# Routing two to four iterations sooner, and the first expert tiles between the last cross-attention iterations, in a one-core decoder layer

## The chip, the cores and the metric

One core of one Trainium2 chip. The metric is the device time of one execution in microseconds. Its engines run their own instruction streams and meet at semaphores: TensorE (PE), VectorE (DVE), ScalarE (ACT), GpSimd (POOL), and SyncE (SP), which here only issues transfers.

## The reference

64 sequences of 64 tokens and width 128 (4096 tokens) pass through causal self-attention (16 heads of 64, one key/value head), cross-attention to a context of width 96, and a mixture of 8 experts of which each token uses 2; each step is followed by a residual sum and a layer norm. The part the change touches:

```python
scores_BSN = jnp.einsum('bsd,nd->bsn', x, Wr) + br
w_BSN = jax.nn.softmax(scores_BSN, axis=-1)
_, idx_BSK = jax.lax.top_k(scores_BSN + biases_N[None, None, :], K)
val_BSK = jnp.take_along_axis(w_BSN, idx_BSK, axis=-1)
val_BSK = val_BSK / jnp.sum(val_BSK, axis=-1, keepdims=True)
...
h_NM2H = jnp.einsum('md,ndh->nmh', x_MD, Wl1) + bl1[:, None, :]
a_NMH, b_NMH = (h_NM2H[..., :H], h_NM2H[..., H:])
y_NMD = jnp.einsum('nmh,nhd->nmd', jax.nn.silu(a_NMH) * b_NMH, Wl2) + bl2[:, None, :]
...
y_MD = jnp.einsum('mn,nmd->md', ew_MN, y_NMD)
```

## The kernel before

The tokens are 32 tiles of 128 (T = 32). A first pass does self-attention tile by tile, a second cross-attention, software-pipelined: in iteration i of `cross` (35 iterations, CROSS_END = T + 3) the engines work on the scores of tile i-1, the probabilities and value product of tile i-2, and the residual and norm of tile i-3. Queries and keys are made for two tiles at once in even iterations, the value side in odd ones. Each engine has its own `cross(i, p)`, and the order of calls in it is the order on that engine. TensorE's (lines 1658 to 1704) goes: first half of the scores (`b_s`), transposes of the probabilities (`b_pT`), products for the next tiles, second half of the scores, value product (`b_y`), routing, more products.

Routing is done in eight groups of four tiles (G = 8, GT = 4). `group_at(i, n)` says which group is due n iterations after its first tile; for group g:
- TensorE: transposes at i = 4g+7 (`route_T`), scores at 4g+9 (`route_scores`), places at 4g+11 (`route_places`);
- VectorE: `route_scores` at 4g+9, `route_pick` (top two) at 4g+10, `route_where` and `route_gates` at 4g+11;
- GpSimd: `route_copy` at 4g+11 (numbers and two copies of the rows of the group into xg), then eight indirect sends of 128 rows each to the buffer xbuf in DRAM at 4g+12 to 4g+14 (`send`).

When group 5 (G_A - 1) is placed, VectorE makes table A: for the first 40 tiles of expert work (J_A = 40) the expert and the first row in xbuf (`table_a_tiles`, `table_a_done`, `table_a_rows`, in iteration 32). Groups 6 and 7 fill the remaining 31 tiles (J = 71), for which table B is made within the expert stage.

The expert stage runs in slots, `slot_tiles` from -2 to J+3. In slot i SyncE loads for tile i+2 the weights of its expert (256 KB, four buffers) and its 128 rows out of xbuf (twelve buffers, of which `hs["x0"]` to `hs["x3"]` allow four at a time), after reading its expert number (eight at a time) and its row number (one at a time). TensorE runs layer 1 of tile i, layer 2 of tile i-2, and transposes the rows of tile i+2; ScalarE does silu and copies, VectorE the gates, GpSimd scatters each result to zbuf (`put`). The last group's routing lies between slots: transposes at slot 4, scores at 6, places at 9, sends at 12 to 19. SyncE waits for those before tile 40. xin, the rows' buffer, lies over the keys' buffer KBD of even tiles, and the tables' scratch behind it.

The stage's entry is guarded on SyncE (lines 428 to 431):

```python
            sent_all(sp, G_A)
            sp.wait_ge(f["tableA"], TABLE_A)
            sp.wait_ge(b["s"], 2 * T)
            slot_tiles(sp, slot_tile)
```

and its load of a tile goes (lines 413 to 423)

```python
                if later(t, JB):
                    sp.wait_ge(hs["L1"], t - JB + 1)
                sp.dma_start(w_now[:, q, :], wl1[:, bass.ds(known[t], 1), :].rearrange("d n h -> d (n h)"))\
                  .then_inc(hs[f"w{q}"], 16)
                row = nc.sync.value_load(row_tab[0:1, bass.ds(t, 1)], min_val=0, max_val=xbuf.shape[0] - P)
                if later(t, JB):
                    sp.wait_ge(hs["T1"], t - JB + 1)
```

After the last tile the two expert results of every token are read back from zbuf, summed with x, normed and stored, in eight groups.

Of the kernel before, what the change touches and what calls it, by code (L numbers as in the profile page):

```python
# [27 lines left out]
ALU = mybir.AluOpType  # L28
ACT = mybir.ActivationFunctionType
AX = mybir.AxisListType  # L30
# [18 lines left out]
def decoder(nc, x, ctxT, g1, wqT, wkvT, woutT, g2, xwq, xwk, xwvT, xwo, bo, wrT, br, wl1, bl1, wl2, bl2, bN, out, xbuf, zbuf):  # L49
# [26 lines left out]
    with ctx:  # L76
# [130 lines left out]
        free = KBD[:, :, :, :, :].rearrange("p a b c d -> p (a b c d)")[:, 4096 - 1600:]  # L207
        past = free[:, 0:J * (NE - 1)].rearrange("p (j e) -> p j e", j=J)
        pastw = free[:, 504:504 + J * (NE - 1)].rearrange("p (j e) -> p j e", j=J)
        over = free[:, 1008:1008 + NE * T].rearrange("p (e t) -> p e t", e=NE)  # L210
        til_to = free[:, 1264:1264 + NE * NE].rearrange("p (a e) -> p a e", a=NE)
# [33 lines left out]
        def staging(n):  # L245
# [14 lines left out]
            "xg", "T_ps", "T", "sc_ps", "sc", "scored", "sh", "ex", "top", "picks", "picked", "before", "pos", "where",  # L260
# [23 lines left out]
        TABLE_A, TABLE_B = 14, 14  # L284
# [7 lines left out]
        def place_bank(g):  # L292
            return 1 if g >= G - 2 else 5
# [7 lines left out]
        def slot_tiles(eng, body):  # L301

            for i in range(-2, J + 4):
                body(i, i % JB)

# [4 lines left out]
        def expert_numbers(eng_type, t, known):  # L310

            n = min(EB, J - t)
            _, values = nc.values_load_multi_w_load_instructions(
                e_tab[0:1, t:t + n], engines=[eng_type], min_val=0, max_val=NE - 1,
                skip_runtime_bounds_check_because="an entry counts which of NE - 1 bounds a tile lies past")
            for k in range(n):
                known[t + k] = values[k]

# [6 lines left out]

        def group_at(i, back):

            return (i - back) // GT if (i - back) % GT == 0 and 0 <= (i - back) // GT < G else None
# [57 lines left out]
        def _(sp):  # L386
# [19 lines left out]
            known = {}  # L406

            def load_rows(t, q):
# [1401 lines left out]
```

## Time and profile before

| | |
|---|---|
| median of 3 runs | 935.6 us (933.85 to 937.73) |
| the profiled execution | 938.14 us, its span 936.2 us |
| busy over the span | PE 89%, DVE 75%, ACT 65%, POOL 51% |
| mean granted TensorE clock | 0.961 of full |
| cross stage (some 440 to 715 us) | TensorE busy 99% |
| hand-over to the experts | about 715 to 750 us |
| expert tiles | 744.5 to 893 us |
| sums, norms, output | 893 to 936 us |

The profile is one execution. Its page shows the span in forty slices with the busy tenths of each engine and the granted clock; the trace behind it gives timelines, waits with the one that released them, and the chain that ended last. Busy time says where an engine could be the bound; the waits of the engine that is the bound say what to remove.

### The profile page before, as it was taken

To read this page: it belongs to the slowest core of one execution; us is meant where nothing else is said; L and a number is where in the kernel's file an instruction comes from. 1 tells how busy PE (TensorE), PEld (TensorE's weight loads), DVE (VectorE), ACT (ScalarE), POOL (GpSimd) and SP (SyncE) were. 2 spreads that over 40 slices of the span, in tenths; PEclk is the share of its full clock that TensorE was granted. 3 is DMA by queue.
4 is the path that set the end of the run, shared out by engine and by line. 5 is a ranking of instruction groups with operands and counts; after the bars stand their busy time and mean duration, and the time that the engine had idled before them with its cause. 6 is when DMAs were issued, how large, how long until landed. Compare 5 with 4: busy or idle time off the path is not lost.

```text
span 936.2 us, 22568 instructions
## 1 busy us (share of the span) xinstructions
PE 830.3 (89%) x7180; PEld 690.4 (74%) x7212; DVE 698.9 (75%) x2101; ACT 604.1 (65%) x1396; POOL 477.8 (51%) x461
## 2 busy tenths in 40 slices
PE   5799999999999988999999999999998588889910
PEld 4577777777777766888888888888886477778810
DVE  5878888888888766889898989898989465334345
ACT  2577767767767765777777777777775265555514
POOL 5366666665675742222244444444444367544553
PEclk9999999999999999999999999999998699999965
DMA  7499999000000000000000000000000266667542
GB/s 243 86 148 150 148 145 109 0 0 0 0 0 0 1 2 5 6 6 6 6 8 26 11 23 12 23 14 20 14 20 12 81 192 200 204 184 208 173 184 90
DMA packets 68806, 64.61 MB, mean 69 GB/s; under 512 B 5638, under 2 KB 54921, under 8 KB 68080
## 3 DMA queue, kind: packets, MB, share of 16 engines
q1 hardware_dynamic: 62016, 51.42, 28.4%
q0 software_dynamic: 4624, 9.61, 2.9%
q10 hardware_dynamic: 2080, 2.49, 0.8%
q8 instruction: 47, 0.77, 0.4%
q14 instruction: 39, 0.32, 0.1%
HBM read 35.37 MB, written 28.58 MB: 68 GB/s over the span
## 4 chain that ended last, share of the span: by engine, by line
PE 69%; DVE 11%; DMA 8%; issue 5%; SPq 4%; POOL 2%; ACT 2%; POOLq 0%; ACTq 0%; DVEq 0%
PE bank L1423 8%; PE bank L1475 7%; PE bank L1424 7%; PE bank L1425 7%; PE bank L1504 6%; PE bank L1510 6%; PE bank L1597 6%; DMA KBD<-xbuf 6%; PE bank L1621 4%; PE bank L1488 3%; PE bank L1722 3%; PE bank L1463 3%; PE bank L1609 3%; DVE KBD L356 2%; DVE L L1066 1%
## 5 line engine op out<-in xcount | busy, mean ns | idle before, releaser
L369 ACT COPY VBD<-bank 64x512 f32<-64x512 f32 x192 | 111.3, 580 | 23.5 <-PE bank L1425 20.7
L509 POOL TENSOR_TENSOR PR<-PR,rL 128x1024 f32<-128x1024 f32 x32 | 61.2, 1911 | 101.9 <-DVE rL L973 101.9
L504 POOL TENSOR_TENSOR rq<-ssq,mhalf 128x17 f32<-128x17 f32 x32 | 99.1, 3097 | 14.5 <-DVE ssq L935 14.4
L541 POOL TENSOR_TENSOR PR<-PR,rL 128x1024 f32<-128x1024 f32 x32 | 60.9, 1902 | 81.7 <-DVE rL L1069 81.5
L602 POOL DMA_INDIRECT zbuf<-PT,KBD x71 | 69.6, 980 | 52.1 <-ACT PT L868 43.7
L1350 DVE SCALAR_TENSOR_TENSOR stage<-bank,b_now,early 128x128 f32<-128x128 f32 x142 | 43.4, 346 | 67.0 <-ACT early L860 59.3
L546 POOL TENSOR_TENSOR rs<-ve,mhalf 128x1 f32<-128x1 f32 x32 | 17.8, 556 | 132.7 <-DVE ve L1082 132.7
L1722 PE MATMUL bank<-xT,w_now 128*128 128x128 f32 x568 | 77.2, 280 | 1.6 <-issue 1.6
L590 POOL DMA_INDIRECT xbuf<-xg,slot x64 | 63.6, 994 | 29.0 <-issue 16.8
L1597 PE MATMUL bank<-KBD,QT 128*64 128x128 f32 x1024 | 70.1, 279 | 5.7 <-DVE PR L1060 5.7
L1475 PE MATMUL bank<-KBD,QT 128*64 128x128 f32 x1024 | 70.1, 279 | 5.1 <-issue 0.7
L1722 PEld LDWEIGHTS bank<-xT,w_now 128*128 128x128 f32 x568 | 72.7, 199 | 2.1 <-issue 2.0
L1597 PEld LDWEIGHTS bank<-KBD,QT 128*64 128x64 f32 x1024 | 56.3, 138 | 20.0 <-issue 17.9
L1621 PE MATMUL bank<-VBD,PT 128*64 128x128 f32 x1024 | 66.4, 285 | 4.3 <-ACT PT L781 3.3
L1475 PEld LDWEIGHTS bank<-KBD,QT 128*64 128x64 f32 x1024 | 54.6, 137 | 20.2 <-issue 20.2
L1621 PEld LDWEIGHTS bank<-VBD,PT 128*64 128x64 f32 x1024 | 58.4, 142 | 12.3 <-issue 5.5
L935 DVE TENSOR_REDUCE ssq<-arena 128x17 f32<-128x1088 f32 x32 | 41.2, 1288 | 33.4 <-ACT arena L670 33.4
L860 ACT ACTIVATE early<-bank,b_now 128x128 f32<-128x128 f32 x142 | 44.4, 364 | 29.5 <-PE bank L1722 26.8
L1504 PE MATMUL bank<-PT,VBD 128*128 128x512 f32 x128 | 63.4, 618 | 0.0
L1510 PE MATMUL bank<-arena 128*128 128x128 f32 x512 | 62.5, 276 | 0.7 <-ACT arena L708 0.7
L692 ACT ACTIVATE PR<-bank 128x512 f32<-128x512 f32 x64 | 38.2, 597 | 38.6 <-PE bank L1475 36.6
L1056 DVE TENSOR_REDUCE mx<-bank 128x8 f32<-128x512 f32 x64 | 44.0, 687 | 25.4 <-PE bank L1597 24.8
(251 smaller groups left out, 2431.3 us busy)
## 6 DMA issues: line engine op xcount, KB each, us to landing
w_now<-in_wl SPq DMA_DIRECT2D x71, 256.0 KB, 3.3
xbuf<-blank SPq DMA_DIRECT2D x1, 17160.0 KB, 125.6
KBD<-xbuf SPq DMA_DIRECT2D x71, 65.0 KB
VBD<-zbuf SPq DMA_DIRECT2D x2, 1024.0 KB, 5.7
out<-X SPq DMA_DIRECT2D x8, 256.0 KB, 2.3
cT<-in_ctxT ACTq DMA_DIRECT2D x16, 96.0 KB, 2.0
zbuf<-PT,KBD POOLq DMA_INDIRECT x71, 3.0
wl_sb<-in_wl POOLq DMA_DIRECT2D x1, 1024.0 KB, 9.4
```

The lines of the kernel that those rows point to most:

```text
L369: u = copy(VBD[h * SEQ:(h + 1) * SEQ, p, s, lo:lo + blocks, :], bank[CHUNK_BANK[c]][s * SEQ:(s + 1) * SEQ, :].rearrange("k (a d) -> k a d" ...
L504: nc.gpsimd.tensor_tensor(rq[:, :], ssq[:, :], mhalf[:, 0:HEADS + 1], ALU.pow).then_inc(a["pow"], 1)
L602: nc.gpsimd.indirect_dma_start(out=zbuf, out_offset=at, in_=yb[:, t % YB, :], in_offset=None, bounds_check=K2 * TOK - 1, oob_is_err=False) ...
L1423: M(out_, l_hi, r_lo, start=True, stop=False)
L1424: M(out_, l_lo, r_hi, start=False, stop=False)
L1425: return M(out_, l_hi, r_hi, start=False, stop=True)
L1475: m = M(bank[6][s * SEQ:(s + 1) * SEQ, k * P:(k + 1) * P], QT[:, p, c * HBLK + k, s * SEQ:(s + 1) * SEQ], KBD[:, p, s, 0, :], start=False, ...
L1504: M(bank[0 if s else 7][:, :], VBD[:, p, s, 0, :], PT[:, s * HW:(s + 1) * HW], start=True, stop=True)\
L1510: m = M(bank[0][:, 0:D], OT[:, k, :], wout_sb[:, k, :], start=(k == 0), stop=(k == NBLK - 1))
L1597: m = M(bank[6][s * SEQ:(s + 1) * SEQ, k * P:(k + 1) * P], QT[:, p, c * HBLK + k, s * SEQ:(s + 1) * SEQ], KBD[:, p, s, c * HBLK + k, :], s ...
L1621: m = M(bank[bk][s * SEQ:(s + 1) * SEQ, 0:D], PT[:, k * P + s * SEQ:k * P + (s + 1) * SEQ], VBD[:, p, s, k, :], start=(k == 0), stop=(k == ...
L1722: m = M(bank[2 + q % 2][:, c * P:(c + 1) * P], w_now[:, q, c * P:(c + 1) * P], xT[:, q % 2, :], start=True, stop=True)
```

## The change

Five things, each in the code of several engines:
- Routing: transposes at 4g+6, scores and picks at 4g+7, places, gates and row copies at 4g+8, sends at 4g+9 to 4g+11, one before and one or two behind GpSimd's other work in an iteration; this for groups 0 to 6. The row copies go from GpSimd to ScalarE. Table A is made in iterations 29 and 30, its scratch moved to other buffers.
- Tiles in turn: slots -2 and -1 run before (TensorE: inside) iteration 32, slots 0 and 1 between 32 and 33, slot 2 between 33 and 34, the rest after.
- SyncE: in slot i the rows of tile i+4, then the weights of tile i+3; row numbers are read eight at a time; it starts when the scores of tile 30 are done, not those of tile 31.
- Last group: VectorE's pieces are cut smaller and spread over slots 7 to 15, table B over 17 to 23, GpSimd's sends of group 6 over iterations 33 and 34 and slots 2 to 10, those of group 7 over slots 16 to 34.
- ScalarE copies xT of tile i+1 at the head of slot i, where it copied that of tile i+2 at its end; in the last even iterations the probabilities' copies go ahead of the second exponential.

```diff
+        LATE_SENDS = {2: 2, 4: 4, 6: 5, 8: 6, 10: 7}
+        LAST_SENDS = {16: 0, 19: 1, 22: 2, 24: 3, 27: 4, 30: 5, 32: 6, 34: 7}
+
+        def T_at(g):
+            return GT * g + 6
+
+        def scores_at(g):
+            return GT * g + 7
+
+        def places_at(g):
+            return GT * g + 8
...
+        def tiles_in_turn(cross, slot_tile, meanwhile):
+
+            for i in range(T):
+                cross(i, i % 2)
+            if not meanwhile:
+                slot_tile(-2, -2 % JB)
+                slot_tile(-1, -1 % JB)
+            cross(T, T % 2)
+            slot_tile(0, 0)
+            slot_tile(1, 1)
+            cross(T + 1, (T + 1) % 2)
+            slot_tile(2, 2)
+            cross(T + 2, (T + 2) % 2)
+            for i in range(3, J + 4):
+                slot_tile(i, i % JB)
...
                 if t % EB == 0:
-                    expert_numbers(mybir.EngineType.SP, t, known)
-                if later(t, JB):
-                    sp.wait_ge(hs["L1"], t - JB + 1)
-                sp.dma_start(w_now[:, q, :], wl1[:, bass.ds(known[t], 1), :].rearrange("d n h -> d (n h)"))\
-                  .then_inc(hs[f"w{q}"], 16)
-                row = nc.sync.value_load(row_tab[0:1, bass.ds(t, 1)], min_val=0, max_val=xbuf.shape[0] - P)
+                    numbers(mybir.EngineType.SP, row_tab, xbuf.shape[0] - P, t, first_row)
+                    expert_numbers(mybir.EngineType.SP, t, expert)
                 if later(t, JB):
                     sp.wait_ge(hs["T1"], t - JB + 1)
                 if later(t, XB):
                     put_wait(sp, t - XB)
-                sp.dma_start(xin[:, t % XB, :], xbuf[bass.ds(row, P), :]).then_inc(hs[f"x{q}"], 16)
+                sp.dma_start(xin[:, t % XB, :], xbuf[bass.ds(first_row[t], P), :]).then_inc(hs[f"x{q}"], 16)
+
+            def load_weights(t, q):
+                if later(t, JB):
+                    sp.wait_ge(hs["L1"], t - JB + 1)
+                sp.dma_start(w_now[:, q, :], wl1[:, bass.ds(expert[t], 1), :].rearrange("d n h -> d (n h)"))\
+                  .then_inc(hs[f"w{q}"], 16)
 
             def slot_tile(i, q):
-                of_tile(load_rows, i, q, -2)
+                of_tile(load_rows, i, q, -4)
+                of_tile(load_weights, i, q, -3)
 
             sent_all(sp, G_A)
             sp.wait_ge(f["tableA"], TABLE_A)
-            sp.wait_ge(b["s"], 2 * T)
-            slot_tiles(sp, slot_tile)
+            sp.wait_ge(b["s"], 2 * (T - 1))
+            for i in range(-4, J + 4):
+                slot_tile(i, i % JB)
...
+            def route_rows(g):
+                act.wait_ge(b["x2"], GT * (g + 1))
+                if g >= 1:
+                    act.wait_ge(f[f"sent{(g - 1) % 2}"], 16 * GT * K2 * ((g + 1) // 2))
+                for k in range(K2):
+                    nc.scalar.activation(xg[:, k, :, 0:D], X[:, g * GT:(g + 1) * GT, :], ACT.Copy).then_inc(f["xg"], 1)
...
+                if (g := due(i, scores_at)) is not None:
+                    score_add(g)
+                    score_shift(g)
+                    score_top(g)
+                    pick_which(g)
+                    pick_mask(g)
+                    pick_count(g)
+                if (g := due(i, places_at)) is not None:
+                    where_sum(g)
+                    where_slot(g)
+                    gate_pair(g)
+                    gate_row(g)
...
+                if i == T:
+                    slot_tile(-2, -2 % JB)
+                    slot_tile(-1, -1 % JB)
```

The last piece stands in TensorE's `cross` behind `b_pT`, ahead of the second half of the scores.

## Rows read from the trace of the kernel before

**Rows 1.** The page: busy tenths of TensorE and its granted clock in forty slices.
```profile
PE   5799999999999988999999999999998588889910
PEclk9999999999999999999999999999998699999965
```
**Rows 2.** Stretches: window, us, busy us of PE, PEld, DVE, ACT, POOL, clock, DMA share, GB/s.
```profile
715.00:734.00 19.00, 13.08 (x116) 11.26 (x115) 15.12 (x42) 6.35 (x11) 10.15 (x10) 0.64 0.06 19
734.00:744.00 10.00, 1.23 (x8) 0.87 (x7) 5.38 (x31) 0.51 (x2) 4.74 (x7) 0.67 0.34 99
...
820.00:850.00 30.00, 26.45 (x208) 23.45 (x209) 11.36 (x44) 16.91 (x59) 13.99 (x15) 1.00 0.64 188
```
**Rows 3.** Timeline of TensorE, 700 to 751: start, us, line, what, [idle before, releaser].
```profile
701.07 1.97 PE L1621 MATMUL bank<-VBD,PT 128*64 128x128 f32 x32
...
706.29 1.09 PE L1597 MATMUL bank<-KBD,QT 128*64 128x128 f32 x16 [0.66 <-DVE PR L1060]
...
715.10 1.09 PE L1597 MATMUL bank<-KBD,QT 128*64 128x128 f32 x16
...
722.20 3.68 PE L1621 MATMUL bank<-VBD,PT 128*64 128x128 f32 x32 [3.28 <-ACT PT L781]
726.94 1.97 PE L1609 MATMUL bank<-ident,PR 128*128 128x128 f32 x8 [1.05 <-POOL PR L541]
729.88 3.68 PE L1621 MATMUL bank<-VBD,PT 128*64 128x128 f32 x32 [0.98 <-DVE r L1073]
733.49 1.29 PE L1638 MATMUL bank<-wr_sb,fT 128*128 128x8 f32 x8
742.69 0.45 PE L1714 MATMUL bank<-ident,KBD 128*128 128x128 f32 x1 [7.91 <-DMA KBD<-xbuf]
...
744.54 1.92 PE L1722 MATMUL bank<-xT,w_now 128*128 128x128 f32 x8
...
750.19 1.06 PE L1722 MATMUL bank<-xT,w_now 128*128 128x128 f32 x8
```
**Rows 4.** Waits in 744 to 895: engine, line, releaser, total us, times, longest.
```profile
PE bank L1714 <- DMA KBD<-xbuf: 14.8, 20, 1.7
```
**Rows 5.** Chain that ended last, 811 to 825: start, us, what.
```profile
815.27 0.33 SPq L416
...
816.41 3.68 DMA KBD<-xbuf
```
**Rows 6.** Timeline of TensorE near the end of the tiles: first layers.
```profile
880.63 1.06 PE L1722 MATMUL bank<-xT,w_now 128*128 128x128 f32 x8
...
885.90 1.06 PE L1722 MATMUL bank<-xT,w_now 128*128 128x128 f32 x8
...
889.27 1.16 PE L1722 MATMUL bank<-xT,w_now 128*128 128x128 f32 x8
```
**Rows 7.** The weights' buffer w_now: landing of its 71 loads.
```profile
DMA to landing us min/median/max: 2.8/3.3/4.3
```
**Rows 8.** Timeline of SyncE around a read of eight numbers.
```profile
753.11 0.33 SPq L423 DMA_DIRECT2D KBD<-xbuf  x1
754.20 0.33 SPq L416 DMA_DIRECT2D w_now<-in_wl  x1
```
**Rows 9.** Timeline of TensorE in slot 9, behind ScalarE's two table loads.
```profile
766.63 0.30 PE L1714 MATMUL bank<-ident,KBD 128*128 128x128 f32 x1 [1.11 <-ACT xT L852]
```
**Rows 10.** Timeline of GpSimd in the expert stage: a put.
```profile
765.90 1.00 POOL L602 DMA_INDIRECT zbuf<-PT,KBD  x1 [0.30 <-issue]
```
**Rows 11.** Chain that ended last, 690 to 940: landing of group 5's last send.
```profile
735.64 2.28 DMA xbuf<-xg,slot
```
**Rows 12.** Timeline of VectorE: first, slowest and last instruction of table A.
```profile
722.50 0.36 DVE L1243 TENSOR_TENSOR KBD<-n_tok,steps_up 128x256 f32<-128x256 f32 x1
...
724.48 2.44 DVE L1260 TENSOR_SCALAR done_from<-done_from 128x8 f32<-128x8 f32 x1
...
729.36 0.18 DVE L1283 CAST row_tab<-row_f 128x40 int32<-128x40 f32 x1
```

More of the change, by code:

```diff
@@ L206, in decoder @@
         row_tab = sb("row_tab", [P, J], mybir.dt.int32)
[L207 to L211, printed above, removed]
+        pastA = stage[:, 0:J_A * (NE - 1)].rearrange("p (j e) -> p j e", j=J_A)
+        pastB = PR[:, 0, 0:(J - J_A) * (NE - 1)].rearrange("p (j e) -> p j e", j=J - J_A)
+        over = xn[:, :, :].rearrange("p a d -> p (a d)").rearrange("p (e t) -> p e t", e=NE)
+        til_to = yS[:, 0:NE * NE].rearrange("p (a e) -> p a e", a=NE)
         xin = KBD[:, :, :, :, :].rearrange("p a b c d -> p (a b c d)")[:, 0:XB * ROW]\
@@ L259, in decoder @@
         f = {n: sem("f_" + n) for n in (
-            "xg", "T_ps", "T", "sc_ps", "sc", "scored", "sh", "ex", "top", "picks", "picked", "before", "pos", "where",
+            "ids", "xg", "T_ps", "T", "sc_ps", "sc", "scored", "sh", "ex", "top", "picks", "picked", "before", "pos", "where",
             "slot_f", "slot", "pex", "gates", "gate", "b2", "sent0", "sent1", "tableA", "tableB")}
@@ L283, in decoder @@
         CONSTS = 19
-        TABLE_A, TABLE_B = 14, 14
+        TABLE_A, TABLE_B = 15, 15
         def T_bank(g):
@@ L298, in sent_all, with numbers, expert_numbers @@
                 eng.wait_ge(f[f"sent{n}"], 16 * GT * K2 * ((groups + 1 - n) // 2))
-        def slot_tiles(eng, body):
-            for i in range(-2, J + 4):
-                body(i, i % JB)
         def put_wait(eng, t):
             eng.wait_ge(hs[f"put{t % YB}"], 16 * (t // YB + 1))
-        def expert_numbers(eng_type, t, known):
+        def numbers(eng_type, table, most, t, known):
             n = min(EB, J - t)
             _, values = nc.values_load_multi_w_load_instructions(
-                e_tab[0:1, t:t + n], engines=[eng_type], min_val=0, max_val=NE - 1,
-                skip_runtime_bounds_check_because="an entry counts which of NE - 1 bounds a tile lies past")
+                table[0:1, t:t + n], engines=[eng_type], min_val=0, max_val=most,
+                skip_runtime_bounds_check_because="an expert is a count of NE - 1 bounds, a row a block within the buckets")
             for k in range(n):
                 known[t + k] = values[k]
+        def expert_numbers(eng_type, t, known):
+            numbers(eng_type, e_tab, NE - 1, t, known)
         def of_tile(fn, i, q, back):
@@ L595, in _ @@
             body(T, 0)
-            for i in range(CROSS_END):
-                cross(i, i % 2)
             def put(t, q):
@@ L801, in cross @@
                         b_q(i, c)
+                if p == 0 and not has(i):
+                    stage_of(b_pT, i, p, 2)
                 stage_of(lambda t, q: b_exp(t, q, 1), i, p, 1)
-                if p == 0:
+                if p == 0 and has(i):
                     stage_of(b_pT, i, p, 2)
@@ L842, in _ @@
             act.wait_ge(b["zero"], 1)
-            for i in range(CROSS_END):
-                cross(i, i % 2)
             def x_copy(t, q):
@@ L1330, in _ @@
             body(T, 0)
-            for i in range(CROSS_END):
-                cross(i, i % 2)
             def b1_column(t, q):
@@ L1706, in _ @@
             pe.wait_ge(b["zero"], 1)
-            for i in range(CROSS_END):
-                cross(i, i % 2)
             def x_T_slot(t, q):
+                if t == 0:
+                    pe.wait_ge(b["u3"], T)
                 pe.wait_ge(hs[f"x{q}"], 16 * (t // JB + 1))
```

210 lines of the change are left out of this document (110 added, 100 removed).

## The prediction

> **What bounds the kernel now.** I read the page's forty slices first. TensorE is busy nine tenths in nearly every slice; the exception is slices 31 and 32 (702 to 749 us), with 8 and 5, where the granted clock falls to 8 and 6 [rows 1]. So there are three parts to price: the cross stage, where TensorE itself is the bound; the hand-over from cross attention to the experts; and the expert stage, four slices of 8 behind them.
>
> The table of stretches puts numbers on the hand-over. From 715 to 734 us TensorE works 13.08 of 19 us at a mean clock of 0.64; from 734 to 744 us it works 1.23 of 10 us [rows 2]. The timeline of TensorE says what each gap waits for [rows 3]: the last scores start at 715.10, the last probabilities wait for GpSimd's normalisation, the last value product starts at 729.88 and takes 3.68 us at the lower clock (1.2 GHz) where the same 32 matmuls took 1.97 us at the higher (2.4 GHz), and then TensorE idles 7.91 us until the first expert rows land. The first layer of tile 0 starts at 744.54, that of tile 3 at 750.19.
>
> In the expert stage the list of waits gives one large cause: TensorE waited 14.8 us in 20 waits for the rows of xbuf [rows 4]. The chain that ended last shows the loop [rows 5]: a first layer ends, SyncE issues that slot's weights (815.27), then reads one row number out of SBUF, issues the rows 1.14 us after the weights (816.41), and the rows take 3.68 us until TensorE can transpose them. Tile 3's first layer starts at 750.19 [rows 3], tile 70's at 889.27 [rows 6]: 139.1 us for 67 tiles, 2.076 us a tile. Near the end, where the loads are not late, the first layers stand 5.27 us apart in three tiles (880.63 to 885.90): 1.757 us a tile [rows 6]. That is TensorE's own work, and loads were still going out then. After tile 70's first layer, 936.2 - 889.27 = 46.9 us follow (last tiles, the sums of both experts, the output), which the change leaves alone.
>
> **Part 1: rows loaded four tiles ahead, numbers read eight at a time.** Before, SyncE issues in slot i the weights and the rows of tile i+2, the rows behind the weights, so behind the first layer of tile i-2. Now it issues in slot i the rows of i+4 (they wait for the transpose of i, done in TensorE's slot i-2) and then the weights of i+3. The rows' lead is four slots, 4 x 1.757 = 7.0 us, against 3.68 us of landing [rows 5] and 0.33 us of issue: 3 us to spare, so the 14.8 us go and nothing of the loads is last. The weights keep their old lead: issued right behind a first layer (1.16 us [rows 6]), needed four slots after that layer began, so 7.0 - 1.2 = 5.8 us for a landing of 3.3 us, 4.3 at most [rows 7]. The single read behind each weight issue goes; eight numbers at once cost at most the 1.09 us between a row issue and the next weight issue at 753.11 and 754.20 [rows 8], now twice in eight slots, 2.2 us in 14. They lie in SyncE's idle time. Sixty-seven tiles at 1.757 us are 117.7 us.
>
> What is late next is worth terms of its own. (a) The last group's routing runs on TensorE between tiles: its eight score matmuls took 1.29 us at the lower clock [rows 3], so with transposes and places 2 us in all. (b) TensorE reads eight expert numbers every eighth slot; no row shows its queue alone. The bounds are nothing and 1.09 us as on SyncE [rows 8], eight times; I take 0.3 us each, nearest to nothing since TensorE's queue runs ahead of its matmuls: 2.2 us. (c) ScalarE swaps its table for the last group's exponentials and back; the row at 766.63 has 1.11 us of TensorE waiting for it with more slack ahead than there will be [rows 9]: 1.6 us, bounds 1 and 3. (d) GpSimd takes 1.30 us a put, issue included [rows 10], and now carries a send in every second or third slot from 16 to 34: 18 + 8 at 1.3 us, 33.8 us of work in 31.6 us. The last send therefore goes out some 3.5 us into slot 34, lands 2.28 us later [rows 11], SyncE reads 16 numbers (2.2 us at most, I take 1.2) and issues the rows of tile 40, with the weights of tile 39 behind them. Rows there at 34 + 10.5 us, wanted at 34 + 8.5 us: 0.5 to 3 us of stall, I take 1.5. Before, these sends were over by slot 19 and cost nothing here. (e) small pieces of the last group on VectorE, spread over more slots than before: 0.5. Slots 3 to 70 become 117.7 + 2 + 2.2 + 1.6 + 1.5 + 0.5 = 125.5 us for 139.1: 13.6 us less.
>
> **Part 2: the first tiles between the last cross iterations.** The groups' routing ends three iterations earlier, so table A is ready in iteration 30 and not at 729.54 [rows 12], the sends of group 5 are issued in iterations 29 to 31 and not at 735.64 [rows 11], and SyncE waits only for the scores of tile 30. The last send then leaves GpSimd near 710 us and lands 2.3 us on, and with the numbers read the first rows go out near 714 and land by 717.5 to 718. TensorE transposes them behind scores and probabilities of 1.1 us each, which start some 1.5 us behind 715.10, so near 719. The 7.91 us wait disappears [rows 3]. Slots 0 and 1 run while VectorE, ScalarE and GpSimd carry tile 31 through its softmax, slot 2 after the last value product. So tile 3 starts one value product and one slot behind the point at which that product can start. That point was 729.88 [rows 3]. Against it: +0.9 us for the last scores of group 6 on TensorE ahead of 715 (before, behind the value product), +1 us for VectorE's eight reads ahead of its maxima (bounds nothing and 1.09 [rows 8]). For it: the 1.0 us that it waited for VectorE's table A, and 0.9 us because the transposes run at the higher clock (0.9 us fewer on 1.97 [rows 3]). Net nothing. Tile 3 starts at 729.9 + 1.97 + 1.76 = 733.6; VectorE's and GpSimd's tail of tile 31 stands between the gates of tiles 2 and 3, for which I add 1 us: 734.6 against 750.19, 15.6 us less. The silu table's load lies in ScalarE's wait for the softmax of tile 31, hidden; uncovered it would cost some 1.1 us, as the two loads did at 766.63 [rows 9].
>
> The last tiles depend on the clock. The lower level came in after TensorE had idled 3.28 us waiting on ScalarE's copies, and the row at 726.94 is still slow (1.97 us for eight transposes) [rows 3]; in the expert stage waits of up to 1.7 us [rows 4] left the clock at full, 1.00 in 820 to 850 us with 3.5 us of idle time [rows 2]. The new gaps before 730 us come out at 0.5 to 1.5 us each, so I take the higher level. The Trainium skill (TensorE: Matmul & The Clock Gate, Part 1: The HAM clock gate) states that an idle array is put back to half rate and must be kept busy to be released; the trace agrees with both halves, and by that rule many short gaps together could do what one long one did. That is rival C.
>
> **Part 3: routing of each group sooner.** The same instructions, two to four iterations earlier, with two row copies a group on ScalarE and no longer on GpSimd, at the end of even iterations, where ScalarE's next work waits for VectorE's maxima anyway; no row has their price there, and the bounds below hold it. In the cross stage the cost is what arrives late at VectorE's maxima. The wait that shows now is 0.66 us at 706.29, behind one group's picks [rows 3]. After the change the picks stand at the end of odd iterations, where VectorE otherwise idles, and places and gates in the even one, as long as the picks were: the same 0.7 us a group, nothing net. The bounds are -0.7 and +1 us a group. Table A is the exception: its chain took 7.04 us (722.50 to 729.54), 2.3 of it one stretched instruction at 724.48 [rows 12], so 4.8 us; 1.7 us fit the free end of iteration 29, 3.0 us stand in 30 ahead of the maxima of 31, some 0.6 us more than the picks now do. With sends spread between GpSimd's other work nothing else waits: +0.6 us, bounds 0 and 3.
>
> **The sum.** 13.6 + 15.6 - 0.6 = 28.6 us less. The profiled run took 938.14 us (936.2 of span and 1.9 around it), 2.5 us over the median. In its own terms: 938.1 - 28.6 = 909.5; against the median, 935.6 - 28.6 = 907.
>
> **Rivals.** A is the forecast: 907, bounds of the unknown terms 900 to 912; chance 0.55.
>
> B: a new limit on the slots. The stretch at 820 us moved 188 GB/s at a DMA share of 0.64 [rows 2]; the same bytes a tile at 1.757 for 2.076 us ask for 222 GB/s. If landings stretch as demand rises, or GpSimd's 1.30 us and its sends set the pace, the slots settle halfway, at 1.92 us: 67 x 0.16 = 11 us, 918. Against it: the 1.757 us pace near the end was held with weights still loading [rows 6], and the spare of the weights is 1.5 us over the longest landing. Chance 0.2. The Trainium skill (DMA: Bandwidth & Descriptors, Latency and other measured facts) puts HBM access at 0.2 us and at 2 us under high load. With its 2 us on top of the longest landing weights would come 0.5 us late, which is B's direction; no row here shows such a rise, the longest landing of 71 being 1.0 us over the median [rows 7].
>
> C: the clock falls anyway in 720 to 735 us. Two value products, two batches of transposes and two first layers at half speed: about 1.7 + 1.7 + 0.9 + 0.9 + 0.9 = 6 us, 913. Chance 0.12.
>
> D: it doesn't do what it says: the first rows come late, because table A or the last sends slip. Transposes of tiles 0 and 1 stand in TensorE's order before the second half of the scores of tile 31, so a late load now holds the cross tail itself. The spare is about 1.5 us (717.5 against 719); 3 us beyond that cost 3 to 5 us, 911. Chance 0.07.
>
> E, the other side: routing in its new places stands on TensorE's path in each of seven groups. At the price of a whole chain of small VectorE instructions, 4.8 us as table A [rows 12], that is 33 us: 935.6 + 33 - 28.6 = 940. It decides from 28.6 / 7 = 4.1 us a group on; the row shows 0.66. Chance 0.03.
>
> The rest, 0.03, is faster than A, with fewer late terms.
>
> **How the numbers follow.** Predicted 907. The range runs from 899 (terms c, d and the 0.7 us a group on the good side) to 920 (B with a little): A, B, C and D within it, 0.9 less the tails of each. A measurement of this kernel can tell about 0.5% from no change, 4.7 us. Faster by more: A to D, 0.95. Within 0.5%: 0.02, where B and E act half. Slower: 0.03.
>
> **What would show it.** Right: no stretch of TensorE idle over 3 us between 715 and 740; first layer of tile 0 near 725 us and of tile 3 near 734; fewer than 4 us of waits for rows; steady first layers 1.76 us apart; one stall of 1 to 3 us near tile 39 or 40; clock at 1.00 in 715 to 740. Wrong: slots at 1.9 us with weights or puts as releasers (B), matmuls of 0.5 us before 735 (C), a wait for KBD inside the last cross iterations (D), or new waits for PR in every group (E).

## The result, and the profile after

The changed kernel took 910.5 us (median of 4 runs, 908.55 to 911.48) beside 934.7 us for the kernel before on the same chip (933.52 to 937.73): a ratio of 0.973, 95% interval 0.970 to 0.976. Forecast were 907 us and a range of 899 to 920. By the medians that is 24.2 us less, where 28.6 us had been forecast. The profiled execution took 910.27 us with a span of 908.4 us: 27.8 us less span than the profile before, which was 2.5 us above its median. The total hides misses of both signs, so here is the span cut at three points, all first layers of expert tiles on TensorE:

| part of the span | before | after | gained | forecast |
|---|---|---|---|---|
| up to the first layer of tile 3 | 750.19 | 737.14 | 13.0 | 15.0 (15.6 less 0.6) |
| tile 3 to tile 70 | 139.1 | 124.6 | 14.4 | 13.6 |
| after tile 70's first layer | 46.9 | 46.6 | 0.3 | 0 |

The page's slices (busy tenths of TensorE, and its granted clock) answer to [rows 1]. The slices are 22.7 us each now, so the hand-over lies in slices 32 and 33 (704 to 749 us). Where 8 and 5 stood, these two read 8 and 8, the clock stays at 9 there, and a dent to 8 has appeared in slice 36 (795 to 818 us), between slices of 9:
```profile
PE   3899999999999998899999999999999889989900
PEclk9899999999999999999999999999999999999955
```
The table of stretches answers to [rows 2] (us, busy us of PE, PEld, DVE, ACT, POOL, clock, DMA share, GB/s). From 734 to 744 us TensorE is busy throughout, at full clock; the stretch at 820 us is full too, and moves 223 GB/s where it moved 188:
```profile
715.00:734.00 19.00, 14.64 (x154) 12.11 (x151) 16.02 (x58) 12.31 (x27) 5.54 (x5) 1.00 0.38 115
734.00:744.00 10.00, 10.00 (x97) 9.08 (x93) 5.43 (x24) 5.08 (x18) 6.32 (x8) 1.00 0.48 133
...
765.00:790.00 25.00, 25.00 (x202) 22.38 (x201) 14.92 (x60) 16.60 (x58) 18.95 (x20) 1.00 0.79 233
790.00:820.00 30.00, 27.65 (x208) 24.46 (x207) 11.41 (x44) 16.89 (x59) 17.34 (x19) 0.94 0.68 203
820.00:850.00 30.00, 30.00 (x242) 26.82 (x241) 13.78 (x53) 19.96 (x69) 16.74 (x18) 1.00 0.75 223
```
The timeline of TensorE at the hand-over answers to [rows 3]. L1668 is scores, L1692 a value product, L1786 the transposes of expert rows, L1796 a first layer:
```profile
710.59 1.09 PE L1668 MATMUL bank<-KBD,QT 128*64 128x128 f32 x16 [1.50 <-DVE PR L1093]
...
719.68 1.09 PE L1668 MATMUL bank<-KBD,QT 128*64 128x128 f32 x16
...
722.50 0.33 PE L1786 MATMUL bank<-ident,KBD 128*128 128x128 f32 x1 [0.71 <-ACT VBD L394]
...
726.73 1.14 PE L1796 MATMUL bank<-xT,w_now 128*128 128x128 f32 x8
...
733.39 1.97 PE L1692 MATMUL bank<-VBD,PT 128*64 128x128 f32 x32 [1.80 <-ACT PT L803]
...
737.14 1.06 PE L1796 MATMUL bank<-xT,w_now 128*128 128x128 f32 x8
```
The 7.91 us wait for the first rows is gone. Their transposes wait for ScalarE's copies (L394), not for a transfer. The last value product takes 1.97 us, not 3.68. It still waits 1.80 us, for ScalarE's copies of the probabilities, and these stand behind the silu of tile 1, for which ScalarE waited 1.44 us for VectorE's bias column. Tile 3 follows the value product after 3.75 us, as forecast (1.97 + 1.76).

In the expert stage the waits for rows, 14.8 us in 20 [rows 4], have become one of 0.9 us, with one of 1.5 us for weights beside it (735 to 868 us; total, times, longest):
```profile
PE bank L1796 <- DMA w_now<-in_wl: 1.5, 1, 1.5
PE bank L1786 <- DMA KBD<-xbuf: 0.9, 1, 0.9
```
Both stand at one place. TensorE's timeline, tiles 38 to 41, then 70; from tile 17 to 38 and from 42 to 69 first layers stand 1.757 us apart:
```profile
801.52 1.06 PE L1796 MATMUL bank<-xT,w_now 128*128 128x128 f32 x8
...
804.07 0.33 PE L1786 MATMUL bank<-ident,KBD 128*128 128x128 f32 x1 [0.89 <-DMA KBD<-xbuf]
805.86 2.00 PE L1796 MATMUL bank<-xT,w_now 128*128 128x128 f32 x8 [1.47 <-DMA w_now<-in_wl]
...
810.99 1.06 PE L1796 MATMUL bank<-xT,w_now 128*128 128x128 f32 x8
...
861.78 1.16 PE L1796 MATMUL bank<-xT,w_now 128*128 128x128 f32 x8
```
From 801.52 to 810.99 are 9.47 us for three tiles that need 5.27: 4.2 us lost. SyncE's timeline says why: after the weights of tile 38 it issues nothing for 6.6 us, then the rows of tile 40, and only behind them the weights of tile 39:
```profile
795.71 0.33 SPq L449 DMA_DIRECT2D w_now<-in_wl  x1
802.32 0.33 SPq L444 DMA_DIRECT2D KBD<-xbuf  x1
802.85 0.33 SPq L449 DMA_DIRECT2D w_now<-in_wl  x1
```
What released it is the last group's last send, which GpSimd issues at 798.24, 3.75 us into slot 34 (four tiles of 1.757 us before 801.52). The chain that ended last has it land 2.71 us later, and SyncE then reads its numbers until 802.1. The row of it in GpSimd's timeline, two puts after the send before it at 794.38:
```profile
798.24 0.97 POOL L621 DMA_INDIRECT xbuf<-xg,slot  x1 [0.31 <-issue]
```

### The profile page after: what moved, and what is told of

The parts are those of the page before. It is cut to its first block, busy times and chain, and to the rows that moved or that the text cites. A ratio compares the mean times of both kernels' runs of the same rounds, so it can differ in the third digit from the quotient of the medians.

```text
span 908.4 us, 22393 instructions
## 1 busy us (share of the span) xinstructions
PE 828.7 (91%) x7212; PEld 681.6 (75%) x7212; DVE 688.3 (76%) x2101; ACT 612.1 (67%) x1412; POOL 461.9 (51%) x445
## 4 chain that ended last, share of the span: by engine, by line
PE 81%; DVE 8%; POOL 3%; issue 3%; DMA 2%; ACT 2%; SPq 0%; POOLq 0%; ACTq 0%; DVEq 0%
PE bank L1494 9%; PE bank L1495 7%; PE bank L1496 7%; PE bank L1546 7%; PE bank L1575 7%; PE bank L1668 6%; PE bank L1581 6%; PE bank L1692 6%; PE bank L1796 6%; PE bank L1559 4%; PE bank L1806 3%; PE bank L1534 3%; PE bank L1680 3%; PE bank L1786 2%; PE bank L1543 1%
## 5 line engine op out<-in xcount | busy, mean ns | idle before, releaser
L394 ACT COPY VBD<-bank 64x512 f32<-64x512 f32 x192 | 111.3, 580 | 32.3 <-PE bank L1496 29.6
L533 POOL TENSOR_TENSOR rq<-ssq,mhalf 128x17 f32<-128x17 f32 x32 | 99.1, 3096 | 14.4 <-DVE ssq L968 14.2
L1415 DVE SCALAR_TENSOR_TENSOR stage<-bank,b_now,early 128x128 f32<-128x128 f32 x142 | 43.5, 346 | 51.8 <-ACT early L891 46.9
L1796 PE MATMUL bank<-xT,w_now 128*128 128x128 f32 x568 | 76.8, 279 | 1.6 <-DMA w_now<-in_wl 1.5
L1668 PE MATMUL bank<-KBD,QT 128*64 128x128 f32 x1024 | 69.9, 278 | 6.6 <-DVE PR L1093 6.6
L1796 PEld LDWEIGHTS bank<-xT,w_now 128*128 128x128 f32 x568 | 73.3, 200 | 2.2 <-issue 2.1
L1668 PEld LDWEIGHTS bank<-KBD,QT 128*64 128x64 f32 x1024 | 55.1, 136 | 22.4 <-issue 20.4
L1692 PE MATMUL bank<-VBD,PT 128*64 128x128 f32 x1024 | 63.0, 276 | 1.8 <-ACT PT L803 1.8
L1692 PEld LDWEIGHTS bank<-VBD,PT 128*64 128x64 f32 x1024 | 55.3, 137 | 9.6 <-issue 5.5
```

What stands on the lines that cost most here:

```text
L394: u = copy(VBD[h * SEQ:(h + 1) * SEQ, p, s, lo:lo + blocks, :], bank[CHUNK_BANK[c]][s * SEQ:(s + 1) * SEQ, :].rearrange("k (a d) -> k a d" ...
L533: nc.gpsimd.tensor_tensor(rq[:, :], ssq[:, :], mhalf[:, 0:HEADS + 1], ALU.pow).then_inc(a["pow"], 1)
L1668: m = M(bank[6][s * SEQ:(s + 1) * SEQ, k * P:(k + 1) * P], QT[:, p, c * HBLK + k, s * SEQ:(s + 1) * SEQ], KBD[:, p, s, c * HBLK + k, :], s ...
L1692: m = M(bank[bk][s * SEQ:(s + 1) * SEQ, 0:D], PT[:, k * P + s * SEQ:k * P + (s + 1) * SEQ], VBD[:, p, s, k, :], start=(k == 0), stop=(k == ...
L1796: m = M(bank[2 + q % 2][:, c * P:(c + 1) * P], w_now[:, q, c * P:(c + 1) * P], xT[:, q % 2, :], start=True, stop=True)
```

## The experiments

Three questions were open: which part of the loads' change brings what (and whether it would have done so alone), what the interleaving and the move of the row copies are worth, and where the 2.5 us went by which tile 3 is later than forecast. In the table "tile 3" is the start of its first layer in us, "3 to 70" the time from there to tile 70's first layer, both in the one profiled execution. The dates of tile 3 carry a spread that no edit made: the first scores of the cross stage start at 440.8 us in the profile before, at 441.4 in the profile after, at 442.2 in its unchanged copy, at 440.0 with the last sends sooner and at 442.9 with the routing ahead of the value product.

| kernel | median us | ratio to before, 95% | tile 3 | 3 to 70 |
|---|---|---|---|---|
| before | 934.7 to 936.7 | 1 | 750.19 | 139.1 |
| + row numbers eight at a time | 931.3 | 0.995 (0.993 to 0.997) | 747.8 | 133.4 |
| + earlier loads | 929.6 | 0.993 (0.991 to 0.995) | 750.0 | 132.0 |
| + both | 926.4 | 0.990 (0.986 to 0.993) | 749.5 | 127.8 |
| + both, sends in every second slot | 923.4 | 0.987 (0.984 to 0.990) | 748.3 | 125.7 |
| after | 910.5, again 910.9 | 0.973, 0.972 | 737.1, 739.5 | 124.6, 124.3 |
| after, tiles not between iterations | 917.4 | 0.979 (0.975 to 0.984) | 743.8 | 124.4 |
| after, row copies on GpSimd | 916.1 | 0.980 (0.975 to 0.984) | 740.2 | 125.1 |
| after, routing ahead of the value product | 908.8 | 0.969 (0.965 to 0.974) | 737.5 | 124.4 |
| after, last sends sooner | 906.4 | 0.969 (0.966 to 0.973) | 737.2 | 120.3 |
| the same, with small edits on VectorE | 906.4 | 0.969 (0.966 to 0.972) | 737.1 | 120.3 |
| the same, and the routing's order | 901.5 | 0.964 (0.962 to 0.966) | 732.1 | 120.8 |

**The loads on the kernel before.** First the numbers alone, with the old lead of two slots:

```diff
                 if t % EB == 0:
-                    expert_numbers(mybir.EngineType.SP, t, known)
+                    numbers(mybir.EngineType.SP, row_tab, xbuf.shape[0] - P, t, first_row)
+                    expert_numbers(mybir.EngineType.SP, t, expert)
...
-                row = nc.sync.value_load(row_tab[0:1, bass.ds(t, 1)], min_val=0, max_val=xbuf.shape[0] - P)
```


> The kernel before with only the row numbers read eight at a time; order and lead of the loads as before. Theory (lead): the rows still leave behind the weights of their own tile, 0.6 us sooner in each round of the loop of four tiles, so about 1.92 us a tile and 10 us less, 925 us, waits for rows still in the trace. Rival (the single read was the cause): 1.76 us a tile as in the run with both, 918 us, no waits left.

Measured 931.3 us, 4.5 us less by the ratio; both expectations had promised more. Rows are still late by the old lead: from tile 42 on a tile takes 1.895 us, and the waits from 740 to 885 us still read
```profile
PE bank L1717 <- DMA KBD<-xbuf: 18.4, 15, 8.0
```
of which 8.0 us are the first rows' wait. Taking the single read away is worth 5.7 us over tiles 3 to 70, less than 0.1 us a tile.

Then the lead alone, the row number still read one at a time:

```diff
             def slot_tile(i, q):
-                of_tile(load_rows, i, q, -2)
+                of_tile(load_rows, i, q, -4)
+                of_tile(load_weights, i, q, -3)
```


> The kernel before with only the lead: rows four tiles ahead and ahead of the weights, row numbers still read one at a time. Theory (lead): SyncE needs some 1.73 us a tile, just below TensorE's 1.757, so 1.76 to 1.80 us a tile, 918 to 920 us. Rival (SyncE's own time becomes the bound without the batch): 1.85 us a tile or more, 923 us or more.

Measured 929.6 us; the last 28 tiles at 1.80 us each. The pace is the theory's (1.76 to 1.80 us), the time the rival's (923 us or more), since the earlier tiles lose more, as in the next run. The lead alone does not reach 1.757 us. Then both, which are the change's two edits on SyncE together, with its start left where it was:

> The kernel before with SyncE's part of the change alone: rows loaded four tiles ahead and ahead of the weights, numbers read eight at a time; routing and hand-over as before, and SyncE still waits for the last scores. Theory (the lead of the rows is what the expert stage lacked): first layers 1.757 us apart, tile 3 to tile 70 in some 121 us where it was 139.1, no stall at tile 40 since these sends end by slot 19; 918 us. Rival (part of the gain of the expert stage came from the late sends and pieces of the last group): 125 us or more for tiles 3 to 70, 922 us or more.

Measured 926.4 us, beside 936.65 for before. Tiles 42 to 70 are at 1.751 us on average, the pace forecast (1.757, and 1.59 for the last), so the loads are no longer the bound there. But tiles 3 to 70 still take 127.8 us: tiles 11 to 28 take 37.0 us where the full change takes 30.3. The rival expectation was met (125 us or more, 922 us or more). The timeline of GpSimd shows what stands there, the last group's copies and eight sends in a row between puts:
```profile
772.82 2.07 POOL L343 TENSOR_TENSOR xg<-X,ones 128x512 f32<-128x512 f32 x2
...
776.40 0.96 POOL L597 DMA_INDIRECT xbuf<-xg,slot  x1 [0.30 <-issue]
...
794.28 0.97 POOL L597 DMA_INDIRECT xbuf<-xg,slot  x1 [0.31 <-issue]
```
To see whether this is the cause, the sends were spread over every second slot and nothing else touched:

```diff
-                if 12 <= i < 12 + GT * K2:
-                    send(G - 1, i - 12)
+                if 12 <= i < 12 + 2 * GT * K2 and i % 2 == 0:
+                    send(G - 1, (i - 12) // 2)
```


> The kernel before with the numbers read on SyncE and rows prefetched at the full distance (926.4 us, tiles 3 to 70 in 127.8 us), with the last group's eight sends in every second slot 12 to 26 instead of eight slots in a row. Theory, GpSimd's eight sends in a row (776 to 795 us) held its other work and with it the rows of tiles 13 to 28: tiles 3 to 70 in 122 to 124 us, the run near 922 us. Rival, VectorE's bunched pieces and row copies are what loses the 6.7 us there: tiles 3 to 70 stay at 127 us or more and the run at 926 us.

Measured 923.4 us; tiles 3 to 70 in 125.7 us, tiles 11 to 28 in 34.3. That lies between the two expectations: the crowd of sends cost about 2.1 us, and some 4 us of loss in those tiles stay. Its list of waits, beside 1.1 us for weights, still has VectorE's pieces of the last group and ScalarE behind them:
```profile
PE bank L1721 <- ACT xT L859: 1.6, 2, 1.1
PE bank L1729 <- DVE stage L1357: 1.6, 2, 1.1
```
The full change, in which those pieces are smaller and further apart and ScalarE's copies moved, has none of them over 0.7 us in all. Which of the two edits removes them wasn't separated.

**The stall at tile 39.** In the changed kernel the last group's sends were put sooner, evenly at every second slot:

```diff
-        LAST_SENDS = {16: 0, 19: 1, 22: 2, 24: 3, 27: 4, 30: 5, 32: 6, 34: 7}
+        LAST_SENDS = {16: 0, 18: 1, 20: 2, 22: 3, 24: 4, 26: 5, 28: 6, 30: 7}
```


> The changed kernel with the last group's eight sends in slots 16, 18 to 30 and not 16 to 34. Theory (the last send holds up the rows of tile 40 and, behind them, the weights of tile 39; the stall also drops TensorE's clock): the 4.2 us between tiles 38 and 41 beyond three slots go, 906 us. Rival (GpSimd's queue is the bound and only shifts): puts run 3 us late, rows wait for puts twelve tiles back, 910 us as the change.

Measured 906.4 us, 4 us less (3.7 us by the ratios, since the two kernels ran on different chips). The four first layers 38 to 41 now stand in line (TensorE's timeline), and tiles 3 to 70 take 120.3 us:
```profile
796.20 1.06 PE L1796 MATMUL bank<-xT,w_now 128*128 128x128 f32 x8
797.96 1.06 PE L1796 MATMUL bank<-xT,w_now 128*128 128x128 f32 x8
```
So the whole of the 4.2 us hung on the date of the last send, and a send in every second slot of GpSimd delays no first layer.

**The interleaving.** Everything of the change but the order of tiles: all slots after the last cross iteration.

```diff
-            if not meanwhile:
-                slot_tile(-2, -2 % JB)
-                slot_tile(-1, -1 % JB)
             cross(T, T % 2)
-            slot_tile(0, 0)
-            slot_tile(1, 1)
             cross(T + 1, (T + 1) % 2)
-            slot_tile(2, 2)
             cross(T + 2, (T + 2) % 2)
-            for i in range(3, J + 4):
+            for i in range(-2, J + 4):
                 slot_tile(i, i % JB)
...
-                if i == T:
-                    slot_tile(-2, -2 % JB)
-                    slot_tile(-1, -1 % JB)
```


> The changed kernel with all expert slots behind the last cross iteration on the four compute engines; routing, SyncE's early start and its lead stay. Theory (the hand-over's gain came from rows and weights being there, the interleaving only fills waits): tile 3's first layer 1 to 4 us later than 737, at a lower clock between 725 and 740, 911 to 914 us. Rival (the interleaving is the gain): 8 us or more later, 918 us or more.

> The changed kernel unchanged, on the chip of the next three, for comparisons of a few microseconds: 910 us, groups of four cross iterations 46.6 us apart.

Measured 917.4 us beside 910.9 for the unchanged copy: 6.5 us, between both expectations. TensorE's timeline:
```profile
729.89 1.64 PE L1674 MATMUL bank<-ident,PR 128*128 128x128 f32 x8 [2.63 <-issue]
732.21 3.68 PE L1686 MATMUL bank<-VBD,PT 128*64 128x128 f32 x32 [0.69 <-ACT PT L797]
...
741.57 0.30 PE L1777 MATMUL bank<-ident,KBD 128*128 128x128 f32 x1 [2.47 <-ACT xT L877]
...
743.84 1.06 PE L1787 MATMUL bank<-xT,w_now 128*128 128x128 f32 x8
```
With nothing put between the iterations TensorE idles 2.63 us and the last value product takes 3.68 us, at half clock. But half clock is not the mark of this edit. The unchanged copy, on the same chip, waits as the changed kernel did and then runs its last value product at half clock too, where the first profile had 1.97 us behind 1.80 us of waiting:
```profile
734.22 3.51 PE L1692 MATMUL bank<-VBD,PT 128*64 128x128 f32 x32 [1.79 <-ACT PT L803]
```
So the clock is no part of what the interleaving is worth in these two profiles: tile 3 starts 4.3 us later without it (743.84 for 739.52), and that is work and waits. The wait of 2.47 us for tile 2 is one of them. ScalarE first waits 1.83 us for VectorE's bias column, then loads the silu table (1.28 us at 739.34), and only behind that and the silu of tile 0 copies xT. The first rows themselves are in place. Of the 13.0 us gained up to tile 3 in the first profile, earlier routing and an earlier SyncE, which no run takes apart, bring 6.3 (750.19 to 743.84). The interleaving brings 4.3, and the rest, 2.4 us, lies between the two profiles of the changed kernel: 1.5 us of clock and a cross stage that starts 0.8 us sooner.

**The row copies.** Back from ScalarE to GpSimd, in the changed kernel:

```diff
+                pool.wait_ge(b["x2"], GT * (g + 1))
+                for k in range(K2):
+                    pool_copy(xg[:, k, :, 0:D], X[:, g * GT:(g + 1) * GT, :]).then_inc(f["xg"], 1)
...
-                if (g := due(i, places_at)) is not None:
-                    route_rows(g)
...
-                if i == 13:
-                    route_rows(G - 1)
```


> The changed kernel with the two row copies of each group back on GpSimd, in the same iteration. Theory (GpSimd's copies stretch VectorE's small instructions beside them, which stood at 0.63 and 0.77 us where they take 0.16 and 0.17 alone, and now right ahead of the maxima): 1 us later a group, 5 to 7 us in all, 916 us. Rival (the move of the copies is worth nothing, as the forecast had it): 910 us.

Measured 916.1 us (913.5 to 920.1), 5.3 us more than the unchanged copy. The number of the theory came true, but not its 1 us a group: sixteen cross iterations, four groups, take 187.65 us (507.17 to 694.82), 46.91 us a group beside 46.64 in the changed kernel. The larger part stands at the hand-over. VectorE's gates of group 6 are stretched there (a CAST of 1.64 us at 729.15 beside GpSimd's normalisation, two instructions of 0.72 and 0.76 us beside its copies). So ScalarE starts the silu of tile 1, behind a wait for VectorE's bias column, 1.5 us later (733.10 for 731.65), and its copies of the probabilities stand behind that. The last value product waits 2.85 us for them, after a wait of 0.91 us for GpSimd's normalisation, and then runs at half clock. Tile 3 starts 0.6 to 3.0 us later than in the two profiles without the edit. The profiled execution is the quickest of its four; how the other three come to be 2.6 to 6.5 us longer than this one isn't shown.
```profile
730.86 1.06 PE L1679 MATMUL bank<-ident,PR 128*128 128x128 f32 x8 [0.91 <-POOL PR L570]
...
734.78 3.11 PE L1691 MATMUL bank<-VBD,PT 128*64 128x128 f32 x32 [2.85 <-ACT PT L806]
```

**The cross stage.** Sixteen iterations (four groups) of the scores' first half, before and after (TensorE's timelines, in this order):
```profile
507.18 1.09 PE L1597 MATMUL bank<-KBD,QT 128*64 128x128 f32 x16
...
691.88 1.09 PE L1597 MATMUL bank<-KBD,QT 128*64 128x128 f32 x16
```
```profile
507.96 1.09 PE L1668 MATMUL bank<-KBD,QT 128*64 128x128 f32 x16
...
694.51 1.09 PE L1668 MATMUL bank<-KBD,QT 128*64 128x128 f32 x16
```
A group takes 46.64 us after and 46.18 before. The 0.46 us are not in the list of waits, from 480 to 700 us (first before, then after):
```profile
PE bank L1597 <- DVE PR L1060: 1.8, 4, 0.5
```
```profile
PE bank L1668 <- DVE PR L1093: 1.2, 5, 0.3
```
TensorE waits less for VectorE than it did. So it was not E's mechanism, and the suspicion fell on TensorE's own order, in which the routing's small matmuls of the even iterations now stand between the value product and the next scores. Moved ahead of the value product:

```diff
-                stage_of(b_y, i, p, 2)
+                if p == 1:
+                    stage_of(b_y, i, p, 2)
+                elif 2 <= i < T + 2:
+                    pe.wait_ge(b["pT"], 2 * (i - 1))
...
+                if p == 0:
+                    stage_of(b_y, i, p, 2)
```


> The changed kernel with TensorE's routing of even iterations ahead of the value product and not between it and the next scores. Theory (the cross stage lost 0.45 us a group because routing now stands between two kinds of matmul that otherwise follow each other closely, value product and scores): 46.2 to 46.4 us a group, 1.5 to 2.5 us less in all, 908 us. Rival (VectorE's maxima are late behind places and gates, whatever TensorE's order): 46.6 us a group and the same waits for PR, 910 us.

The same two rows, and the hand-over behind them:
```profile
508.29 1.09 PE L1668 MATMUL bank<-KBD,QT 128*64 128x128 f32 x16
...
691.79 1.09 PE L1668 MATMUL bank<-KBD,QT 128*64 128x128 f32 x16
...
707.88 1.91 PE L1668 MATMUL bank<-KBD,QT 128*64 128x128 f32 x16 [1.79 <-DVE PR L1093]
...
732.28 3.42 PE L1692 MATMUL bank<-VBD,PT 128*64 128x128 f32 x32 [1.79 <-ACT PT L803]
```
A group takes 45.88 us, 0.76 us less than in the changed kernel. That the order matters is shown; why a batch costs more in one place than in the other is not. Yet the run gained only 2.0 us by the medians (its four runs lie from 905.6 to 910.6, and the profiled one is the slowest): in the profile both waits at the hand-over are 1.79 us, and both are followed by matmuls at half clock. The second of them is so in the unchanged copy too.

**All together.** The sends sooner, two small edits that shorten VectorE's work at the hand-over, and (in the second kernel) the routing's order:

```diff
-                of_tile(b1_column, i, q, -1)
+                if i == -1:
+                    b1_column(0, 0)
+                    b1_column(1, 1)
+                elif i != 0:
+                    of_tile(b1_column, i, q, -1)
```
The other edit moves `table_a_done` one iteration sooner.

> The same without the reordering on TensorE. Theory: 905 to 906 us, with a group's period of 46.6 us; the run with the reordering is 3 to 4 us shorter. Rival (the hand-over gives the reordering's gain back): the two within 1 us.

> The changed kernel with four small edits: the last group's eight sends in every second slot 16 to 30 (906.4 us alone), TensorE's routing work ahead of the second matrix in even iterations (period of a group 45.9 instead of 46.6 us, 908.8 us alone, its 5 us given back at the hand-over), the second bias column made one slot sooner on VectorE, and the wait for the first layer table put one iteration sooner. Theory: the gains add once the two VectorE waits at the hand-over (1.8 us each in the run with the reordering alone) shrink: 906.4 less about 5 us of the cross stage, plus about 1 us of waits that stay, 901 to 903 us, tile 3's first layer near 734, tiles 3 to 70 near 120.3 us. Rival: the hand-over is bound by VectorE's chain of the last iterations and ScalarE's copies, not by TensorE, so that the 5 us are given back again: 905 to 907 us, with waits of 3 us or more or half clock between 703 and 735 us.

Measured 906.4 and 901.5 us. The small edits bring nothing by themselves (906.4 us with and without them); with the order, 5.0 us. In the two profiles the last value product starts 3.5 us sooner (728.34 for 731.82, from the same point at 507 us within 0.4): that is the cross stage. The other 1.6 us up to tile 3 are the clock: the last value product starts behind the same wait in both, and runs at full clock in one and at half in the other (first the kernel with the old order, then the one with the new). Since the changed kernel itself shows both levels in two profiles, this part isn't shown to be the new order's.
```profile
731.82 3.53 PE L1696 MATMUL bank<-VBD,PT 128*64 128x128 f32 x32 [1.70 <-DVE r L1106]
```
```profile
728.34 1.97 PE L1696 MATMUL bank<-VBD,PT 128*64 128x128 f32 x32 [1.70 <-DVE r L1106]
...
732.09 1.06 PE L1805 MATMUL bank<-xT,w_now 128*128 128x128 f32 x8
```
At 901.5 us this version is 9 us quicker than the changed kernel, and 34 us quicker than the one before on the same chip.

## Why the prediction was right, and where it was not

**Part 1, the sum of the slots: 124.6 us against 125.5, right by two misses that cancel.** The base, 67 tiles at 1.757 us, held exactly. Term (b), 2.2 us for TensorE's number reads, was worth nothing: every first layer from tile 42 to 69 stands 1.757 us after the last, every eighth included. The value to take between the bounds was the lower one itself. Terms (a), (c) and (e) were 4.1 us; tiles 3 to 16, in which all of that work stands, lost 2.9 us. Term (d) is the one mis-sized: 4.2 us for 1.5. The date was well worked out. The forecast had the rows of tile 40 come 1 us later than they did; they held TensorE for 0.9 us. What failed is the clause "with the weights of tile 39 behind them", which was written down and given no price. Those weights left 0.53 us behind the rows and landed 3.0 us later, which is another 1.5 us of waiting; and the two waits in a row put the clock down, so that the first layer, the second and the transposes of that slot cost some 1.6 us more. A stall must be priced with all that is queued behind the waiting instruction and with the clock that it costs.

**Part 2, the hand-over: right from the last scores on, and in the clock by luck.** The forecast had these scores at 716.6 (715.1, 0.6 for table A, 0.9 for group 6) and tile 3 at 734.6, 18.0 us on; in the trace they start at 719.68 and tile 3 17.5 us later. The first rows went out at 716.69, 2.7 us later than forecast, and were no limit (rival D), since TensorE was later too. The last value product waited 1.80 us, over the 0.5 to 1.5 us foreseen for the gaps. The clock stayed at 1.00 from 715 to 744, as forecast, but the reason given, that gaps of this size leave it up, does not hold: in the unchanged copy the same waits ended in half clock, 1.5 us of it, and the granted clock was 0.83 from 734 to 744. Rival C happened there in small, one value product and not the 6 us of its sum. The silu table's load was costed at nothing, as hidden. With the interleaving it is hidden in the main: the copy of xT behind it keeps TensorE waiting 0.85 us. Without it the wait is 2.47 us, of which the load is 1.28; the price named for losing the cover, 1.1 us, was right for the load.

**Part 3, "nothing net": the step that failed.** Only VectorE was examined, since its wait was the one that showed. The price came on TensorE, which was 99% busy there: 0.46 us a group by the new places of the routing's matmuls, about 2 us by iteration 30, inside the bounds of -0.7 and +1 us a group, but not at the value taken. With 0.6 us that the profile was late already at the first scores of the cross stage (441.40 for 440.77), and what table A cost beyond its price, that is most of the 3.1 us by which the last scores came later than forecast. The experiment with the other order turns it into a gain of 0.3 us a group over before. Table A cost 1.50 us of waiting where 0.66 had stood, 0.8 us more; 0.6 had been forecast. Its chain as the trace has it (VectorE, its first instruction behind the copies, and the maxima that it held):
```profile
705.59 0.41 DVE L1309 TENSOR_SCALAR done_to<-til_end 128x8 f32<-128x8 f32 x1
...
709.03 0.69 DVE L1089 TENSOR_REDUCE mx<-bank 128x8 f32<-128x512 f32 x1
```
stood 3.4 us ahead of the maxima of 31, where 3.0 had been worked out. The row copies were given no price on ScalarE, and no wait of TensorE from 480 to 700 us is put down to ScalarE; but the forecast gave no gain to their leaving GpSimd, and put back there they cost 5.3 us.

**The rivals.** B, a slot of 1.92 us, did not happen: 233 GB/s at a share of 0.79, more than the 222 at which it should have set in, with TensorE busy for all of 25 us. On the kernel before, though, Part 1 alone meets a limit at tiles 11 to 28, in which the crowd of sends has a share; the other parts of the change remove it, which the sum had taken for granted in term (e). E fell with its 0.3 us waits.

## What to carry to other kernels

Where an engine waits in its queue for a late event, price everything queued behind that instruction, and the clock as well: here 0.9 us of late rows became 4.2 us, and seven of eight sends put one to four slots sooner took all of it back. On an engine that is busy throughout no list of waits shows what a moved instruction costs; measure the period of its loop before and after, and try the other order. Filling the seam between two stages with the next stage's first work paid 4 us up to tile 3 and 6.5 us in the whole; that it holds the clock as well is not to be counted on while a wait of 1.8 us is left. And where two profiles of one kernel differ in the clock of a stretch, run the unchanged kernel again before a change of clock is put down to an edit.

## What the runs showed of the hardware

The granted clock is not settled by the length of the last gap, nor by the kernel. Six profiles have their last value product behind a wait of 1.70 to 1.80 us. It ran at full clock (1.97 us) in two: the changed kernel (1.80 us of waiting) and the last version (1.70). It ran at half clock, in the main or throughout, in four: the unchanged copy (1.79, then 3.51 us), the one with the sends sooner (1.80, then 3.29), the one with the routing's order (1.79, then 3.42) and the one with the small edits (1.70, then 3.53). The first of each list are the same kernel, with the same waits before within 0.05 us. Where a gap of 2.63 us or more had come shortly before, it took 3.68 us (before, and without interleaving) or 3.11 (row copies on GpSimd). The Trainium skill (TensorE: Matmul & The Clock Gate, Part 1: The HAM clock gate) says of the rise at a kernel's start that its point varies from run to run. These rows show the like of the fall, and no run here gives the rule by which it comes.

Elementwise work on GpSimd stretches some of VectorE's instructions. In the stretch 480 to 700 us, where GpSimd's row copies ran beside them, two small instructions of the gates took 628 and 764 ns; with the copies on ScalarE, 163 and 174 ns (VectorE's groups by line: busy us, mean ns, idle before; first before, then after):
```profile
L1237 DVE TENSOR_TENSOR xg<-exk,er 128x8 f32<-128x8 f32 x5 | 3.8, 764 | 0.2
L1231 DVE TENSOR_TENSOR es<-exk 128x4 f32<-128x4 f32 x5 | 3.1, 628 | 0.2
```
```profile
L1289 DVE TENSOR_TENSOR xg<-exk,er 128x8 f32<-128x8 f32 x5 | 0.9, 174 | 0.2
...
L1281 DVE TENSOR_TENSOR es<-exk 128x4 f32<-128x4 f32 x5 | 0.8, 163 | 0.2
```
In the profile before each of these instructions ends within 0.1 us of the end of one of the two copies (483.82 and 0.63 us, the first copy 483.37 and 1.03 us; 484.70 and 0.76 us, the second copy until 485.43). With the copies put back on GpSimd in their new place it was a CAST with one input that took 454 ns for 171. The Trainium skill (GPSIMD Engine Reference, Key points) has VectorE and GpSimd share their SBUF interfaces, with contention for VectorE's instructions with two SBUF inputs or in a two-port mode; the first pair agrees, and whether the CAST ran in such a mode no row here shows.
